# Attention state as 32x32 blocks, another opening and other places for the weight unit, in a linear-attention and gated-FFN kernel

## The reference, cut to what matters

```python
h = layernorm(x)
q, k = rotate(silu(h @ Wq)), rotate(silu(h @ Wk));  v = h @ Wv;  gate = h @ Wg1 @ Wg2
for each chunk:                                     # S: one 32x32 state per head
    scores  = (qi @ ki.T) * D                       # decay mask, per head
    o       = scores @ vi + (qi * decay_q) @ S
    S       = lam_C * S + (ki * decay_k).T @ vi
x1 = x + (group_rmsnorm(o * sigmoid(gate)) * w) @ Wo
```

## Time and profile before

| | before |
|---|---|
| median of 3 runs | 1309.8 us |
| the profiled execution, its own time | 1306.11 us |
| its span (first to last instruction) | 1304.0 us |
| PE busy | 1278.6 us, 98% of the span |
| DVE / ACT / POOL busy | 942.3 / 475.8 / 435.6 us |
| granted clock of PE over the span | 0.997 of full |

### The profile page before, as it was taken

One profiled execution on the slowest core, in us unless ns is written; L12 is line 12 of the kernel. 1 busy time (PEld: TensorE's weight loads), 2 busy tenths in 40 slices (PEclk: granted clock), 3 DMA queues, 4 the chain that ended last, 5 costly groups with the idle time before them and its releaser, 6 DMA issues.

```text
span 1304.0 us, 19587 instructions
## 1 busy us (share of the span) xinstructions
PE 1278.6 (98%) x6796; PEld 1053.0 (81%) x6796; DVE 942.3 (72%) x1641; ACT 475.8 (36%) x799; POOL 435.6 (33%) x360
## 2 busy tenths in 40 slices
PE   8999998998999999999999999999999999999998
PEld 5788877877778888888888888888888888888887
DVE  6888888888777676766767676767677676667655
ACT  4433433335433333333333333333333333333331
POOL 2443545367432324132222423241322223232410
PEclk9999999999999999999999999999999999999999
DMA  9000000000010000101001100001010010000003
GB/s 324 8 1 9 18 9 1 1 2 1 1 49 25 25 24 24 32 16 32 28 21 32 32 24 24 24 24 32 16 32 24 24 32 30 26 24 24 25 9 121
DMA packets 21774, 40.17 MB, mean 31 GB/s; under 512 B 2660, under 2 KB 2916, under 8 KB 21604
## 3 DMA queue, kind: packets, MB, share of 16 engines
q1 hardware_dynamic: 21060, 39.47, 9.2%
q10 hardware_dynamic: 672, 0.13, 0.0%
HBM read 35.40 MB, written 4.19 MB: 30 GB/s over the span
## 4 chain that ended last, share of the span: by engine, by line
PE 89%; DVE 7%; issue 1%; DMA 1%; POOL 1%; SPq 0%; ACT 0%; DVEq 0%; POOLq 0%
PE bank L1340 15%; PE bank L1343 15%; PE bank L1342 15%; PE bank L1194 12%; PE bank L1196 12%; PE bank L1195 12%; PE bank L1208 2%; PE bank L1284 1%; DMA acc<-x_dram 1%; PE bank L1301 1%; DVE nt_t L624 1%; PE bank L1312 1%; DVE nt_t L626 1%; DVE nt_v L620 1%; DVE xol L831 1%
## 5 line engine op out<-in xcount | busy, mean ns | idle before, releaser
L883 DVE TENSOR_TENSOR acc<-acc,bank 128x512 f32<-128x512 f32 x248 | 169.1, 682 | 129.4 <-PE bank L1196 129.3
L1194 PE MATMUL bank<-wdh,hh 128*128 128x512 f32 x512 | 199.3, 389 | 0.0
L1196 PE MATMUL bank<-wdh,hl 128*128 128x512 f32 x512 | 199.2, 389 | 0.0
L1195 PE MATMUL bank<-wdl,hh 128*128 128x512 f32 x512 | 199.2, 389 | 0.0
L1340 PE MATMUL bank<-xoh,wgh 128*128 128x512 f32 x448 | 175.9, 393 | 0.6 <-DVE cxa L891 0.6
L1340 PE MATMUL bank<-xoh,wuh 128*128 128x512 f32 x448 | 175.1, 391 | 0.7 <-ACT cxa L477 0.7
L1343 PE MATMUL bank<-xoh,wgl 128*128 128x512 f32 x448 | 174.5, 390 | 0.0
L1343 PE MATMUL bank<-xoh,wul 128*128 128x512 f32 x448 | 174.4, 389 | 0.0
L1342 PE MATMUL bank<-xol,wuh 128*128 128x512 f32 x448 | 174.3, 389 | 0.0
L1342 PE MATMUL bank<-xol,wgh 128*128 128x512 f32 x448 | 174.3, 389 | 0.0
L899 DVE TENSOR_TENSOR hl<-hx,hh 128x512 fp32r<-128x512 f32 x128 | 113.4, 886 | 51.5 <-ACT hh L484 51.1
(11 more groups left out here) (161 smaller groups left out, 2331.1 us busy)
## 6 DMA issues: line engine op xcount, KB each, us to landing
stg<-packed_dram SPq DMA_DIRECT2D x48, 256.0 KB, 2.6
stg<-scales_dram SPq DMA_DIRECT2D x48, 256.0 KB
out_dram<-acc SPq DMA_DIRECT2D x16, 256.0 KB, 2.0
acc<-x_dram SPq DMA_DIRECT2D x3, 1024.0 KB, 14.2
w_in<-wq_dram SPq DMA_DIRECT2D x2, 512.0 KB, 5.1
w_in<-wk_dram SPq DMA_DIRECT2D x2, 512.0 KB, 6.9
w_in<-wv_dram SPq DMA_DIRECT2D x2, 512.0 KB, 8.7
w_in<-wo_dram SPq DMA_DIRECT2D x2, 512.0 KB, 10.9
```

The lines of the kernel that those rows point to most:

```text
L883: V.tensor_tensor(row, row, BY[j % 2][:], ALU.add).then_inc(y_add, 1)
L1194: pe.matmul(dst, w_h, x_h, start=start, stop=False)
L1195: pe.matmul(dst, w_h, x_l, start=False, stop=False)
L1196: return pe.matmul(dst, w_l, x_h, start=False, stop=stop)
```

## The change

Four edits in one.

**State.** `st` becomes [128, 4, 32]: each partition holds, for each of four groups, only its own head's 32 columns. `inter` becomes 16 products of a 32x32 block with 32 rows of `qdT`, `kv_product` 16 products of 128 rows with 32x32 results; `state` becomes one operation on 128x128 elements, and `scaled` works on a quarter of the elements.

```diff
 def inter():
     for g in range(KT):
-        ins = pe.matmul(BO[:, P * g:P * g + P], st[:, g, :], qdT[:, g, :],
-                        start=(g == 0), stop=False, skip_group_check=True)
+        for r in range(QB):
+            rows = slice(HD * r, HD * r + HD)
+            ins = pe.matmul(BO[rows, P * g:P * g + P], st[rows, g, :], qdT[rows, g, :],
+                            start=(g == 0), stop=False, skip_group_check=True)
 ...
 def kv_product(b, c, dst):
     for g in range(KT):
-        ins = pe.matmul(dst[:, P * g:P * g + P], kd[:, P * g:P * g + P],
-                        vs[:, c % 2, P * g:P * g + P], start=True, stop=True)
+        for r in range(QB):
+            head = slice(HD * (QB * g + r), HD * (QB * g + r) + HD)
+            ins = pe.matmul(dst[HD * r:HD * r + HD, HD * g:HD * g + HD], kd[:, head],
+                            vs[:, c % 2, head], start=True, stop=True)
 ...
 def state(b, c, src):
-    for r in range(QB):
-        rows, cols = slice(32 * r, 32 * r + 32), slice(32 * r, 32 * r + 32)
-        kv = src[rows, :].rearrange("p (g n) -> p g n", g=KT)[:, :, cols]
-        (add or copy into st[rows, :, cols])
+    kv = src[:, 0:KT * HD].rearrange("p (g d) -> p g d", g=KT)
+    (add or copy into st[:], one instruction)
```

**Unit places.** The tiles are `UNIT_BITS` (3, 6, 9) to (5, 7, 9), `UNIT_SCALE` (5, 7, 10) to (6, 8, 10), `UNIT_PARTS` (6, 8, 11) to (7, 9, 11). Within a tile ACT makes the high parts ahead of `ot_copy(t)` instead of behind `square(t)`, and POOL makes the low parts around `scaled` instead of at the tile's end:

```diff
 def tile(b, c):                       # POOL
     rope_b_(t + 1, (c + 1) % CHUNKS)
     if c == CHUNKS - 1:
         decay_k_(b + 1, 0, t + 1)
+    unit_lo(t, 0)
     if 1 <= c < CHUNKS - 1:
         scaled(b, c)
+    unit_lo(t, 1)
     if c + 1 < CHUNKS - 1:
         decay_k_(b, c + 1, t + 1)
     if t in UNIT_SCALE[:2]:
         unit_sums(UNIT_SCALE.index(t), UNIT_SCALE.index(t))
-    if t == UNIT_PARTS[GATE]:
-        wide_lo(GATE, wgh, wgl)
 ...
```

More of the change, by code:

```diff
@@ L358, in xt_hi_ @@
                     return
+                if t == 2:
+                    act.wait_ge(v_ps, 1)
+                    A(xth[:], BO[:].rearrange("p (k t) -> p k t", k=KT), ACT.Copy
+                      ).then_inc(xt_hi, 1)
+                    return
                 act.wait_ge(v_ps, t)
@@ L423, in _ @@
             weight_hi(2, 2, 1)
+            act.wait_ge(s_g2, 16)
+            A(g2s[:], g2_in, ACT.Copy).then_inc(s_ghi, 1)
             xt_hi_(1)
@@ L426, in _ @@
             gate_low(0)
-            act.wait_ge(s_g2, 16)
-            A(g2s[:], g2_in, ACT.Copy).then_inc(s_ghi, 1)
+            norm1(2, 2)
             v_copy(0, 0)
             tanh_gate(0)
-            norm1(2, 2)
             silu_qk(1)
-            gate_low(1)
             def x1t_hi_(g):
@@ L475, in tile @@
                             wide_hi(u, u, wuh if u else wgh, piece)
+                ot_copy(t)
+                square(t)
+                if t == 1:
+                    norm1(t + 3, 3)
             def copy(dst, src, signal):
@@ L747, in stats2 @@
                 dve.wait_ge(ln2_done, last)
-                newton(s_ntl, ln2[:, rows, 1], last - first, r2[:, rows], NT * (5 + n), 1.0,
+                newton(s_ntl, ln2[:, rows, 1], last - first, r2[:, rows], NT * (4 + n), 1.0,
                        LN_EPS)
@@ L1144, in x1_sums, with unit_lo @@
                 nc.gpsimd.tensor_tensor(x(T4), x(B21), x(T2), ALU.subtract).then_inc(xs_done, 1)
+            def unit_lo(t, piece):
+                if t == UNIT_PARTS[GATE]:
+                    wide_lo(GATE, wgh, wgl, (piece,))
+                if t == UNIT_PARTS[UP]:
+                    wide_lo(UP, wuh, wul, (piece,))
+                if t == UNIT_PARTS[DOWN]:
+                    down_lo(DOWN, (piece,))
             def tile(b, c):
@@ L1376, in _ @@
             v_project(0)
-            pe.wait_ge(s_glo, 2)
-            gate2(0)
             q_ready(1)
@@ L1381, in _ @@
                 q_part(k, x_of(1))
+            pe.wait_ge(s_glo, 2)
+            gate2(0)
             def tile(b, c):
@@ L1406, in tile @@
                     scores(g)
-                x_transpose(t + 2)
+                if not at_start(b, c):
+                    x_transpose(t + 2)
                 if at_start(b, c):
```

94 lines of the change are left out of this document (45 added, 49 removed).

## The result

The changed kernel takes **1296.15 us** (median of 4 runs, 1295.15 to 1296.87). Before, run beside it, took 1310.04 (1309.06 to 1310.69). The ratio is 0.9894, 95% interval 0.9877 to 0.9911. The profiled execution took 1295.76 us against 1306.11, its span 1293.7 against 1304.0, so 10.3 of the 13.9 us can be looked for in the two traces. Both profiled executions had a mean granted clock of 0.997.

A forecast was written before the change was run, and what follows sets the result against it. PE was taken to bound the FFN's untouched 934 us, leaving gains to the first 370. Unit places -7.9, opening -3.4, strips 0 and passage -1.5 made -12.8: 1306.1 to 1293.3, plus 3.7 gives 1297.0 us, range 1288 to 1305.

The forecast's parts named there:

- Unit places: Attention tiles: moving the weight units' low parts removes 9.85 us in tiles 7, 9, 12, gives 1.9 back: -7.9.
- the one that gave tile 8 +1.9: Tile 8: `unit_bits` held by POOL delays the reduction, the chain meets the rotation's halves, and the tile becomes 1.9 us too long.
- In tile 10 my 0: Tile 10: the reduction falls about 1.2 us into the tile and its chain ends in time, so it costs 0.
- Opening: Before tile 1: PE's waits for the gate's split and for x of tile 2 go, 1.9 and 1.46 us: -3.4.
- late Wv at most 1.9 as a bound: Opening: Wv issued behind 0.75 MB more could make `otl` late by up to 1.9 us.
- the opening gives nothing, since Wv comes late: Rival on the opening: no gain there, time 1300.4 us; chance 0.10.
- Strips in the tiles: Attention tiles: -1.2 us from `kv_product` and +1.2 from `inter`, 12 of each, sum 0.
- `kv_product` at 0.9: Strips on PE: `kv_product` takes 0.9 us from start to start, where it took 1.00.
- follows its columns: Rival on strips: `kv_product` takes 0.25 us for 0.9, 7.8 less in 12 tiles, time 1289.2; chance 0.15.
- serial ones would take 4.0 by the estimate of the prediction: Rival on strips: those of `inter` can't overlap and take 4.0 us, not 1.08; +35, time 1332; chance 0.07.
- Passage: Passage after the tiles: shorter `scaled` and `state` cut PE's 1.0 us wait for POOL's sums and the first `normed`: -1.5.
- the 3.7 us by which the profiled execution of before lay under its median: Last step of the sum: added to the 1293.3 forecast for the profiled execution, giving the median 1297.0.

The follow-up runs named there:

- e8: The changed kernel with low parts back at the end of POOL's list and high parts behind `square` on ACT, new tiles kept: 1306.06 us, ratio 0.9975.
- e2: The kernel before with the new unit places and statistics alone: 1300.2 us, ratio 0.9931.
- e1: The kernel before with the new opening alone: 1309.33 us, ratio 1.0.
- e9: The changed kernel with the opening of before, so state blocks and unit places only: 1296.73 us, ratio 0.99.
- e4: The changed kernel with Wv issued ahead of Wg2 and x of tiles 2 and 3: 1293.39 us, ratio 0.9875.
- e5: e4 with POOL's very first rotation waiting until the `newton` chain of tiles 2 and 3's statistics is through: 1290.3 us, ratio 0.9861.
- e7: The changed kernel with `o_back` of chunks 0 to 2 moved behind the first quarter of the Q projection: 1294.87 us, ratio 0.9882.
- e11: e5 with the late `o_back` of e7 in the tiles of chunks 0 to 2 except tiles 9 and 13: 1288.65 us, ratio 0.9839.
- e3: The kernel before with the 32x32 state (strips) alone: 1303.67 us, ratio 0.9947.

## Why the prediction was right in its sum and not in its terms

**Unit places: the cause right, what comes back wrong.** Predicted -7.9, measured -9.96 in the tiles of the trace, and 9.9 back in the median with the place in the tile undone (e8). Alone (e2) they gave 9.6 in the median but 6.4 between the traces, since 2.4 came back in tile 10 and 0.5 in tile 8. The reading of one POOL operation holding one DVE operation held in every chain looked at here. The failed step is the one that gave tile 8 +1.9: I took the reduction to start 2.5 into the tile and it started at 1.95, so `sq` started 0.02 us before the rotation where I let the chain pay 2.0 for it. In tile 10 my 0 was right by luck: I put the reduction 1.2 into the tile, it started at 1.89, and `sq` was 0.05 us ahead of the rotation. A term that a half us decides in this way should have had both values, not a middle.

One reading was incomplete too. I found three tiles too long and took the rest to be alike; tile 1 lasts 19.27 us before, 0.6 more than other chunk-1 tiles. It is 18.66 in the changed kernel, 18.67 with the strips alone and 19.28 with each of the other two parts alone, so this 0.6 belongs to the strips.

**Opening: the step that failed.** Predicted -3.4, nothing measured (e1, e9), and +2.93 in the profiled pair. I saw that the waits for `g2s` and x would go, and they went. I gave late Wv at most 1.9 as a bound and took 0: ACT split Wv 4.7 us later than before (18.16 for 13.49), after a wait of 4.11. And I missed a second thing that the order of instructions showed: with `s_glo` gone from POOL's first rotation, this starts beside the chain that ends in `otl`. I had called that a stall elsewhere in the same prediction. e4 and e5 take the two away one after the other, and tile 1 starts 2.98 and then 3.23 us earlier (2.8 and 3.1 in the medians). So the idea of the opening was good for about 6 us (1290.3 in e5, 1296.73 without it in e9), and its two side effects cost that much. The rival "the opening gives nothing, since Wv comes late", at 0.10, was right on the size; late Wv is one of the two causes.

**Strips in the tiles: 0 nearly right, and by luck.** They gave about 1.0 us there (0.6 in tile 1, 0.4 in the others), since one price that was too high met a wait that I did not see. I took `kv_product` at 0.9; it takes 0.48 from start to start, 0.41 where a product stands right behind it. `inter` at 1.08 took 1.00. The rival "follows its columns" was nearer the truth of the price (0.25), but not of the time: PE then waits 0.42 for ACT's copy. I priced the work and did not ask what is late next behind it. e7 and e11 get it back.

The Trainium skill ("TensorEngine Tiling (Array Packing)", Gotcha 1) says that different row tiles can't be at one PSUM bank at once. The strips of `inter` do that, each into its own output partitions, and 32 passes took 1.00 us, where serial ones would take 4.0 by the estimate of the prediction. So this trace shows nothing of it for strips of this kind. The floor of about 25 ns from start to start that the Trainium skill gives ("TensorE: Matmul & The Clock Gate", "Wait — 56ns, not 53.3ns?") doesn't hold for these four strips side by side: 0.41 us for 32 passes are 12.8 ns each.

**Passage: predicted -1.5, measured -2.3** (bounds 0 to -3.0), and only half for my reason. PE's waits for POOL there, in the changed kernel:

```profile
PE bank L1344 <- POOL ws L1140: 1.0, 1, 1.0
...
PE bank L1344 <- POOL stg L1139: 0.2, 1, 0.2
```

in the kernel before, and in e9, which has the same state and units as the changed kernel:

```profile
PE bank L1332 <- POOL stg L1142: 1.6, 1, 1.6
```
```profile
PE bank L1333 <- POOL stg L1135: 1.6, 1, 1.6
```

The wait of 1.0 that I meant to shorten is as it was. What belongs to the strips is tile 14: it is 1.18 shorter in the changed kernel, 1.17 in e3, and not shorter in e1 and e2 (24.67 and 24.65 for 24.69). The other 1.1 us come with the second wait, of 1.6 for `stg`, which I had not counted and which is 0.2 in the changed kernel. It doesn't follow the change: it is 0.2 in e1, e2 and e3, of which e1 and e2 have the old `scaled`, and 1.6 again in e9. Why it comes and goes stays open.

**From the trace to the median.** I added the 3.7 us by which the profiled execution of before lay under its median. That was luck, not reasoning: 10.35 us went between the profiled executions, 13.9 between the medians, so my 1293.3 for the profiled one was 2.5 too low and the 3.7 on top 3.3 too high. The kernel before ranges from 1304.5 to 1312.9 over all its runs here, the changed one over 1.7 us in its four.

Most of this goes with the granted clock, of which every run has the mean over its span. Of the 47 executions of the kernel before in the groups of runs of the experiments:

| mean granted clock | executions | us | mean |
|---|---|---|---|
| 0.997 | 18 | 1304.5 to 1309.0 | 1307.0 |
| 0.996 | 7 | 1308.2 to 1309.0 | 1308.7 |
| 0.995 | 4 | 1308.3 to 1310.2 | 1309.5 |
| 0.993 | 8 | 1309.7 to 1311.1 | 1310.4 |
| 0.992 | 10 | 1310.8 to 1312.9 | 1311.7 |

The profiled execution of before was one of the best kind, with two stretches at 1.2 GHz; executions near the median have a lower mean, and so more of them. This also accounts for most of why the parts add up to more than the whole (9.6 and 6.1 alone, 13.9 together). At 0.997, and so with one value of the clock, the kernel before took 1307.0 in the mean, e3 1303.67 and e2 1301.3 (one execution each), and the changed kernel 1295.9 (three). That is, as an estimate from few executions, 3.3 for the strips, 5.7 for the units and 11.1 for all, near the 10.3 of the traces; the 2.1 between are about what tile 10 gives only when both are there (2.4). The rest of each median goes with the clock: e2's other three executions have 0.998 to 0.999, two of e3's 0.999, and the kernel before never more than 0.997. A long wait of PE can bring the low clock and cost time by itself, so the table doesn't say which comes first. Why an execution gets more or fewer such stretches, and where those lie that were not profiled, stays open. The wait that the new unit places took out of tile 9 had such a stretch behind it.

That the opening of before can wait 1.74 or 3.79 us at `gate2(0)`, with the clock after it, is shown (before, e9); it makes 1.8 us at tile 1.

## What to carry to other kernels

Look for tiny operations on VectorE that take a us or two, and put GpSimd's long operations where no such chain runs: placing the low parts of three weight units that way was worth about 10 of the 13.9 us here. When a wait is taken off a queue, look up what now starts earlier and beside what; when an operation gets cheaper, what is late next behind it. Where the chain behind an idle TensorE can't be shortened, a few idle products ahead of the wait's end kept its clock, for 1 to 2 us. And before two medians are compared, compare the granted clock of their executions: here a gain of 9.6 in the median was some 6 at an equal clock.

## What the runs showed of the hardware

- Each operation of POOL held one operation of DVE's chain, and the chain's next one then met POOL's next. In e8 four held four (2.11, 2.03, 1.22, 1.21 us where 0.17 are needed). It goes both ways, as the starts fall: in tile 8 of the changed kernel `sq` started 0.02 us before POOL's rotation and was not held (0.69), and the rotation took 4.04 for 2.54.
- `kv_product`: 128 rows, 32 columns each way, four strips side by side, 12.8 ns per pass. With 128 columns moving, `intra` takes 28 (0.90 for 32).
- At one place of the opening PE's idle times from 1.97 to 3.79 us went with a stretch at 1.2 GHz, but for one of 2.16 in e8, and those from 1.63 to 1.76 did not (the table above). Elsewhere idle times from 1.3 to 2.7 us went either way. In e4 seven products then ran 0.43 us apart in place of 0.23, and with two at its edges the stretch cost 1.6 us.
- The mean granted clock tells executions of one kernel apart: 1307.0 us at 0.997 and 1311.7 at 0.992 in the kernel before.
- A transfer issued behind 0.75 MB of others in the full first 20 us came late by about 5 us (ACT split Wv from 18.16 on, 13.49 before and 13.21 in e4), and the median of its two transfers from issue to landing went from 8.7 to 13.5 us.
